# Two tiles at a time in seven half-size products, in a grouped expert GEMM followed by a folded FFN GEMM

## The reference

```python
# x: (128, 64, 1024), ids: (128,), weight: (16, 1024, 1024), all float32
y = jnp.einsum('bsi,boi->bso', x, weight[ids])
h = jnp.einsum('bsd,nrd->nbsr', y, lora_A)                       # 8 adapters of rank 16
lora = jnp.einsum('nbsr,nor->bso', h, lora_B * (2 * lora_weights)[:, None, None])
out = x + (jnp.einsum('bsd,od->bso', y, W) + bias) + lora
```

## Time and profile before

| what | value |
|---|---|
| median of 3 runs | 1487.84 us (1487.71 to 1491.29) |
| profiled execution, its own time | 1489.22 us |
| span of its instructions | 1487.5 us |
| PE busy | 1472.7 us, 99% of the span |
| DVE busy | 797.7 us, 54% |
| ACT busy | 409.0 us, 27% |
| POOL busy | 464.6 us, 31% |
| matmul instructions | 6266 in the trace |
| moved by DMA | 258 MB, 173 GB/s over the span |

### The profile page before, as it was taken

How to read it: one execution, slowest core, us unless ns; L and a number is a source line. 1 busy time by engine, 2 the same in 40 slices (tenths; PEclk the granted TensorE clock), 3 DMA queues, 4 the chain that set the end, 5 groups by cost and what they waited for, 6 DMA issues and landing times.

```text
span 1487.5 us, 29739 instructions
## 1 busy us (share of the span) xinstructions
PE 1472.7 (99%) x6266; PEld 1177.4 (79%) x6267; DVE 797.7 (54%) x1213; ACT 409.0 (27%) x537; POOL 464.6 (31%) x651
## 2 busy tenths in 40 slices
PE   8999999999999999999999999999999999999998
PEld 4887888888888887878888888888888888888887
...
GB/s 254 325 187 236 218 222 157 198 183 194 196 215 215 154 197 197 157 248 232 184 147 149 131 141 131 148 132 143 144 135 141 137 144 136 140 145 135 140 148 103
DMA packets 172716, 258.02 MB, mean 173 GB/s; under 512 B 31616, under 2 KB 135552, under 8 KB 172672
## 3 DMA queue, kind: packets, MB, share of 16 engines
q1 hardware_dynamic: 128896, 138.62, 36.0%
q10 hardware_dynamic: 23360, 73.28, 16.7%
...
HBM read 181.93 MB, written 75.50 MB: 173 GB/s over the span
## 4 chain that ended last, share of the span: by engine, by line
PE 91%; DMA 2%; issue 2%; DVE 2%; SPq 2%; ACT 0%; POOLq 0%; DVEq 0%; POOL 0%; ACTq 0%
PE ps L844 29%; PE ps L851 29%; PE ps L848 29%; PE ps L886 2%; PE ps L889 2%; DMA w_place<-in_L_cond_weight_dram 2%; SPq L244 1%; SPq L222 1%; DVE w_lo L652 1%; DVE rows_by L587 1%; DMA x_raw<-in_x_dram 0%; DVE x_turn L683 0%; POOLq L210 0%; SPq L210 0%; ACT w_hi L422 0%
## 5 line engine op out<-in xcount | busy, mean ns | idle before, releaser
L844 PE MATMUL ps<-w_hi,x_both 128*128 (+1 forms) x2000 | 507.8, 395 | 1.1 <-issue 1.1
L851 PE MATMUL ps<-w_lo,x_both 128*128 (+1 forms) x2000 | 507.1, 395 | 0.0
L848 PE MATMUL ps<-w_hi,x_both 128*128 (+1 forms) x2000 | 507.1, 395 | 0.0
L683 DVE STREAM_TRANSPOSE x_turn<-x_raw 128x256 f32<-128x256 f32 x544 | 193.7, 414 | 515.3 <-DMA x_raw<-y_scr 456.6
L844 PEld LDWEIGHTS ps<-w_hi,x_both 128*128 128x128 f32 x2000 | 375.2, 188 | 93.9 <-issue 2.5
L848 PEld LDWEIGHTS ps<-w_hi,x_both 128*128 128x128 f32 x2000 | 375.4, 188 | 91.3
L851 PEld LDWEIGHTS ps<-w_lo,x_both 128*128 128x128 f32 x2000 | 375.4, 188 | 91.3
L222 POOL DMA_DIRECT2D x_raw<-in_x_dram x560 | 299.1, 534 | 381.3 <-DVE x_turn L683 206.8
L430 ACT ACTIVATE x_both<-x_turn 128x512 fp32r<-128x512 f32 x272 | 168.3, 631 | 770.7 <-DVE x_turn L683 702.8
L405 POOL TENSOR_TENSOR rows_by<-rows_by,w_place 128x1024 f32<-128x1024 f32 x64 | 153.2, 2394 | 620.5 <-DMA rows_by<-in_x_dram 620.5
L690 DVE TENSOR_TENSOR x_both<-x_turn,x_both 128x512 fp32r<-128x512 f32 x272 | 180.8, 691 | 91.8 <-ACT x_both L430 86.1
...
## 6 DMA issues: line engine op xcount, KB each, us to landing
...
x_raw<-in_x_dram POOLq DMA_DIRECT2D x560, 64.0 KB, 3.9
x_raw<-y_scr SPq DMA_DIRECT2D x512, 64.0 KB, 2.4
rows_by<-in_x_dram SPq DMA_DIRECT2D x128, 256.0 KB, 3.7
out_dram<-rows_by ACTq DMA_DIRECT2D x126, 256.0 KB, 3.0
...
```

The lines of the kernel that those rows point to most:

```text
L683: last = nc.vector.transpose(x_turn[h][:, :, s * TOK:(s + 1) * TOK].rearrange("p t (j m) -> p m t j", m=2), x_raw[raw][:, 2 * s:2 * s + 2, ...
L844: mm(ps[b][:, cols], x_hi[b][:, t, :], hi[t], start=t == 0, stop=False)
L848: mm(ps[b][:, cols], x_lo[b][:, t, :], hi[t], start=False, stop=False)
L851: last = mm(ps[b][:, cols], x_hi[b][:, t, :], lo[t], start=False, stop=t == KT - 1)
```

## The change

Seen as 2x2 blocks, a pair of tiles (256 rows: the even rows of four samples and the odd ones, by two halves of the contraction) is multiplied by the folded matrix (two halves of the contraction by two halves of the columns) in seven products of blocks in place of eight. The operands are A11, A12, A22 of y and four sums S1 to S4; on the other side B11, B21, B22 of the folded matrix and four sums T1 to T4. A product of blocks has 3 x 4 = 12 matmuls of the same size as before, so a pair has 84 where two tiles had 96. Each goes into a PSUM bank of its own.

- **Sums of the weights.** In 16 pieces during the first stage: POOL loads a piece of `weff` (4 loads), DVE turns it and makes four sums (`turn_piece`), ACT rounds, DVE subtracts (`split_piece`), POOL stores it to DRAM (2 stores). Between the stages SP loads the sums from there: T2 over B12, which is not needed, in 8 loads of 256 KB as soon as the folded matrix is ready and the pieces are stored; T1, T3 and T4 into the other half of `w_hi` and `w_lo` when the last slot is done, in 6 loads of 1 MB. All are made of runs of 512 bytes.
- **Operands.** Per pair DVE makes four transposes of 128x512, four sums of 128x512 and seven subtractions of 128x512; ACT rounds seven of 128x512.
- **Results.** The seven products go to four quarters of the output. ACT copies the first from PSUM (`copy_common`); DVE adds two more to it in turn (`take_common`) and five straight into `out_rows`; POOL adds the three common sums to rows in four additions of 128x512 (`add_first`, `add_second`) beside the two bias additions of 128x1024 (`add_bias`).
- **Order.** DVE turns pair p + 1 (`turn_pair`) before it takes anything of pair p, and makes the subtractions between the takes. SP's loads of y stay as they are, eight for each tile; `load_rest` has four loads for each pair after one wait for `out_stored` of the pair two before.
- The end is not cut in halves any more: the last pair is stored in four stores of 256 KB. The scratch for POOL's DMA descriptors goes from 8192 to 2048 bytes.

```diff
+    T1, T2, T3, T4 = range(4)
+    A11, A12, S2, S1, S3, S4, A22 = range(7)
...
-                sp.wait_ge(x_turned, turned)
+                if isinstance(group, int) and group == 0:
+                    sp.wait_ge(x_turned, 2 * (t + SLOTS) - (2 * RING - 2))
+                elif u % 2 == 0:
+                    sp.wait_ge(y_turned, group * 8 + (4 * (u // 2) - 4))
...
+            def load_rest(p, q, stores=None):
...
+                samples = [entry(sp, order_sample, 4 * p + s, SAMPLES - 1) for s in range(4)]
                 if stores is not None:
...
-                    sp.wait_ge(out_stored[b], stores)
-                for h in range(2):
-                    sp.dma_start(stage[b][h * TOK:(h + 1) * TOK, :], one(x, samples[h])).then_inc(rest_loaded[b], 16)
+                    sp.wait_ge(out_stored[q], stores)
+                for s in range(4):
+                    sp.dma_start(out_rows[q][s * BLK:(s + 1) * BLK, :, :],
+                                 x[bass.ds(samples[s], 1)].rearrange("a (j m) n -> (a j) m n", m=2)).then_inc(rest_loaded[q], 16)
+
...
+
+            sp.wait_ge(w_ready, ranks * CHUNKS + CHUNKS)
+            sp.wait_ge(piece_stored, 32 * PIECES)
+            for comb, held in ((comb_hi, w_hi), (comb_lo, w_lo)):
+                for c in range(CHUNKS // 2):
+                    load_comb(T2, held[:, bass.ds(par, 1), CHUNKS // 2 + c, 0:KH, :].rearrange("p a t m -> p (a t) m"),
+                              comb[c * 4:(c + 1) * 4, :, T2 * P:(T2 + 1) * P].rearrange("g p f -> p g f"))
+            load_rest(0, 0)
+
+            sp.wait_ge(x_ready, 2 * SLOTS)
+            sp.dma_start(bias_sb[:, :], bias.rearrange("(a n) -> a n", a=1).to_broadcast([P, D])).then_inc(bias_loaded, 16)
+
+            sp.wait_ge(tile_done, SLOTS)
+            for i in (T1, T3, T4):
+                for comb, held in ((comb_hi, w_hi), (comb_lo, w_lo)):
+                    at = T_AT[i] // P
+                    load_comb(i, held[:, bass.ds(other, 1), at // KT:at // KT + 2, :, :].rearrange("p a c t m -> p (a c t) m"),
+                              comb[:, :, i * P:(i + 1) * P].rearrange("g p f -> p g f"))
+            for b in range(2):
+                sp.wait_ge(stored[b], 16 * (SLOTS // 2))
+            load_rest(1, 1)
...
+                    for h in range(2):
+                        load_y(g * RING + (RING + 2 * q + h), g + 1, 2 * q + h)
+                    load_rest(g * 2 + (q + 2), q, g * 64 + 64)
+
+            with sp.Fori(0, PAIRS // 2 - 1) as g:
+                for q in range(2):
+                    out_step(g, q, False)
...
+            def load_piece(i):
+                rows = weff.rearrange("(h r) n -> r h n", h=2)[bass.ds(i * BLK, BLK), :, :]
+                for q in range(QUADS):
+                    pool.dma_start(piece_raw[BLK * q:BLK * (q + 1), :, :],
+                                   rows[:, :, q * SEG:(q + 1) * SEG]).then_inc(piece_loaded, 16)
+
+            def store_piece(i):
+                pool.wait_ge(piece_ready, i + 1)
+                for comb, held in ((comb_hi, piece_hi), (comb_lo, piece_lo)):
+                    pool.dma_start(comb[bass.ds(i, 1)].rearrange("a p f -> (a p) f"),
+                                   held[:, :, :].rearrange("p b m -> p (b m)").bitcast(f32)).then_inc(piece_stored, 16)
+
+            for b in range(RING):
+                load_x(2 * RING + b, b)
+            load_piece(0)
+            with pool.Fori(3, SLOTS // RING) as g:
                 for b in range(RING):
                     load_x(RING * g + b, b)
+                store_piece(pool.snap(g - 3))
+                pool.wait_ge(piece_stored, g * 32 - 64)
+                load_piece(pool.snap(g - 2))
...
+            def add_bias(p, q):
+                pool.wait_ge(rest_loaded[q], (p // 2 + 1) * 64 if isinstance(p, int) else p)
+                for m in range(2):
+                    nc.gpsimd.tensor_tensor(out_rows[q][:, m, :], out_rows[q][:, m, :],
+                                            bias_sb[:, :], ALU.add).then_inc(rest_biased, 1)
+
+            def add_rows(p, q, i, m, half):
+                rows = out_rows[q][:, m, half * HALF:(half + 1) * HALF]
+                nc.gpsimd.tensor_tensor(rows, rows, common[q][i][:, :], ALU.add).then_inc(common_added, 1)
+
+            def add_first(p, q):
+
+                pool.wait_ge(rest_biased, p * 2 + 2)
+                pool.wait_ge(common_copied, p + 1)
+                add_rows(p, q, 0, 0, 0)
+                pool.wait_ge(taken, p * TAKES + 2)
+                add_rows(p, q, 1, 0, 1)
+
+            def add_second(p, q):
+
+                pool.wait_ge(taken, p * TAKES + 5)
+                for half in (1, 0):
+                    add_rows(p, q, 2, 1, half)
+
+            add_bias(0, 0)
+            add_first(0, 0)
+            add_bias(1, 1)
+            add_second(0, 0)
+            with pool.Fori(0, PAIRS // 2 - 1) as g:
+                add_first(g * 2 + 1, 1)
+                add_bias(g * 64 + 128, 0)
...
+            def round_op(p, q, i):
+
+                if not isinstance(p, int) or p > 1:
+                    if i in (A11, S2):
+                        act.wait_ge(common_added, p * ADDS + {A11: 1 - 2 * ADDS, S2: -ADDS}[i])
+                elif p == 0 and i in (S4, A22):
+                    act.wait_ge(tile_done, SLOTS)
+                made = {A11: (y_turned, 1), A22: (y_turned, 2), A12: (y_turned, 4),
+                        S1: (y_summed, 1), S2: (y_summed, 2), S3: (y_summed, 3), S4: (y_summed, 4)}
...
+            def copy_common(p, q):
+                act.wait_ge(product, p * OPS + 1)
+                nc.scalar.activation(common[q][0][:, :], bank[A11], COPY).then_inc(common_copied, 1)
+
+            def store_out(p, q):
+                samples = [entry(act, order_sample, 4 * p + s, SAMPLES - 1) for s in range(4)]
+                act.wait_ge(taken, p * TAKES + TAKES)
+                act.wait_ge(common_added, p * ADDS + ADDS)
+                for s in range(4):
+                    act.dma_start(out[bass.ds(samples[s], 1)].rearrange("a (j m) n -> (a j) m n", m=2),
+                                  out_rows[q][s * BLK:(s + 1) * BLK, :, :]).then_inc(out_stored[q], 16)
+
+            def out_step(p, q, last=False):
+                copy_common(p, q)
+                if not last:
+                    for i in range(OPS):
+                        round_op(p + 1, 1 - q, i)
+                store_out(p, q)
+
+            out_step(0, 0)
+            with act.Fori(0, PAIRS // 2 - 1) as g:
+                out_step(g * 2 + 1, 1)
+                out_step(g * 2 + 2, 0)
...
+            def turn_piece(i):
+                dve.wait_ge(piece_loaded, i * (16 * QUADS) + 16 * QUADS)
+                for h in range(2):
+                    nc.vector.transpose(piece_turn[:, h, :, :].rearrange("p k (t j) -> p (k t) j", j=BLK),
+                                        piece_raw[:, h, :].rearrange("p (t i) -> p t i", i=BLK)).then_inc(piece_turned, 1)
+                dve.wait_ge(piece_turned, i * 2 + 2)
+                b11, b21, b12, b22 = [piece_turn[:, h, k, :] for h in range(2) for k in range(2)]
+                t = [piece_sum[:, k, :] for k in range(4)]
+                tt(t[T1], b12, b11, ALU.subtract).then_inc(piece_summed, 1)
+                tt(t[T3], b22, b12, ALU.subtract).then_inc(piece_summed, 1)
+                dve.wait_ge(piece_summed, i * 4 + 1)
+                tt(t[T2], b22, t[T1], ALU.subtract).then_inc(piece_summed, 1)
+                dve.wait_ge(piece_summed, i * 4 + 3)
...
+            def split_piece(i):
+                dve.wait_ge(piece_rounded, i + 1)
+                tt(piece_lo[:, :, :], piece_sum[:, :, :], piece_hi[:, :, :], ALU.subtract).then_inc(piece_ready, 1)
...
+            def turn_pair(p, q):
+
+                if not isinstance(p, int):
+                    dve.wait_ge(product, p * OPS - OPS)
+                elif p == 1:
+                    dve.wait_ge(tile_done, SLOTS)
                 else:
-                    dve.wait_ge(tile_done, SLOTS + t + 1)
-                tt(stage[t % 2][:, cols], ps[t % RING][:, cols], stage[t % 2][:, cols], ALU.add
-                   ).then_inc(out_added if half else end_added, 1)
+                    dve.wait_ge(piece_stored, 32 * PIECES)
+                for i, m, k in ((A11, 0, 0), (A22, 1, 1), (S3, 1, 0), (A12, 0, 1)):
+                    nc.vector.transpose(
+                        block[q][i][:, :, :].rearrange("p t (s j) -> p s t j", j=BLK),
+                        y_raw[q][:, :, m, k * KH * BLK:(k + 1) * KH * BLK].rearrange("p s (t i) -> p s t i", i=BLK)
+                        ).then_inc(y_turned, 1)
+                dve.wait_ge(y_turned, p * 4 + 4)
+                b = [block[q][i][:, :, :] for i in range(OPS)]
+                tt(b[S1], b[S3], b[A22], ALU.add).then_inc(y_summed, 1)
+                dve.wait_ge(y_summed, p * 4 + 1)
+                tt(b[S2], b[S1], b[A11], ALU.subtract).then_inc(y_summed, 1)
```

(75 more changed lines are left out.)

247 lines of the change are left out of this document (144 added, 103 removed).

## The result

The kernel takes 1632.08 us, the median of 4 runs (1630.42 to 1633.21); the kernel before beside it 1487.78. The ratio is 1.096 [1.094, 1.098]: slower by 9.6%, far above the range of 1489 to 1548 that was forecast. The profiled execution has a span of 1631.4 us.

What follows compares the result with a forecast made beforehand. SP's queue, at 22.7 us a pair above PE's 19.6, was to pace the second stage: 829 + 28 x 22.7, then 15.0, 1.9, 24.9 and 5.8, span 1512.2, median 1513 us; 8-in-10 range 1489 to 1548.

Steps and rivals of the forecast that it cites:

- PE's 90 us saved: Second stage: 84 matmuls a pair for 96, 19.6 us for 22.4, 90 us less PE work in all.
- Rival 3: Something larger, 512-byte packets near 66 ns each or a first stage losing its lead: 1545 us and above, chance 0.06.
- First stage. I take nothing; up to 5.: First stage: the pieces' added work, 41 us on DVE, stays covered; nothing added, up to 5 us.
- Between the stages: Turn to second stage: loading the sums takes 39 us, PE loses 33 us, y(3)'s loads begin at 829.
- The step: Second stage: SP's queue takes 22.3 to 23.5 us a pair, taken as 22.7, for 28 steps.
- The loop that the forecast worked out as 21.8: Second stage, through stores and y loads: 43.6 us for two pairs, 21.8 each, so it just doesn't bind.
- 17.6 us from y's landing to the last take: Term of the loop through the stores: DVE's and POOL's work from y landing to last take, 17.6 us.
- rival 2: Second stage: DVE and POOL hold each other up; 21.5 us for 17.6, step 23.7, median 1541 us, chance 0.30.
- SP's pace: Second stage: SP's queue, full with its own issuing, sets 22.7 us a pair, 3.1 us above PE's 19.6.
- The end: After y(31)'s loads begin: issue 15.0, landing 1.9, PE 24.9, take and four stores 5.8 us.
- PE's matmuls keep their 0.233 us.: Sign that the forecast is right: each second-stage matmul still takes 0.233 us.
- The strided operands: Second stage: moving operand of four of seven products in runs of 32; between nothing and 2.8 us a pair, taken as nothing.

Runs made afterwards that it cites:

- run 1: Changed kernel without all work on the 16 weight pieces (loads, transposes, sums, rounding, stores): 1541.4 us, ratio 1.036 to the kernel before.
- run 5: run 2 with the two stores of each piece issued by ACT instead of POOL: 1552.4 us, ratio 1.044 to the kernel before.
- run 2: Changed kernel with the piece's raw tile in its own block, its load issued after the second x load: 1565.1 us, ratio 1.052 to the kernel before.
- run 4: Changed kernel with POOL adding the bias to only 8 of 1024 columns of each row: 1593.4 us, ratio 1.071 to the kernel before.
- run 6: Changed kernel with POOL adding the next pair's bias after the present pair's last common additions: 1592.8 us, ratio 1.072 to the kernel before.
- run 12: Changed kernel plus a tail timing single DVE and POOL operations without transfers: SBUF subtraction 0.69 us alone, 1.74 beside POOL.
- run 9: run 8 with SP issuing the rest rows between the loads of a pair's two y tiles: 1489.5 us, ratio 1.001 to the kernel before.
- run 8: Changed kernel with piece's own block, piece stores on ACT, y one pair ahead and bias last: 1494.1 us, ratio 1.005 to the kernel before.
- run 13: run 9 with each pair's 16 y loads merged into 4: 1436.8 us, ratio 0.965 to the kernel before.

## Why the prediction was wrong

The direction was right: PE's 90 us saved are lost elsewhere. The time was not, and the direction came out in part by something the sum had at nothing. By the marks, the changed kernel without the first stage's 82.5 us would be at 1549.6 (an estimate), just above the range. Rival 3 named "a first stage that loses its lead", at 0.06.

- **"First stage. I take nothing; up to 5."** This step failed, with 82.5 of the 119.2 us. The pieces' work was sized well: transposes 0.77 us for two (forecast 0.7), sums 0.28 to 0.29 each, the subtraction 0.68, and runs 1 and 5 put what shows of it at 5.9 us. POOL's queue was named, "6 DMAs and a store's landing", and dismissed because x loads run slots ahead. The step asked who waits for what is *behind* the wait, and not who waits for the piece's load itself. That is DVE, in order, with everything of the stage behind it. Runs 2 and 5 take 81.6 us away by moving a buffer and two issues.
- **Between the stages**, 62.5 forecast and 68.0 measured: the size was near. Its waits are seen in TensorE's 11.5 and 8.5 us for T2 and T1, in POOL's 39.2 for the bias row, which is issued behind T2, and in DVE's 16.2 for POOL. Pair 0's last product ends at 897.3, 48.3 us after the start, for 52.6. Then DVE's last take waits 11.3 us for POOL and ends at 907.08, 58.1 us after the start, for 53.3: POOL's bias for pair 1 stands ahead of pair 0's last sums and waits 16.5 us for its rows. That is most of the 5.5 us; no run tried it.
- **The step**, 22.7 for 23.48. The term in the sum was SP's own issuing, and it was too high: the y loads of a pair with the reads between them cost 13.37 us for 15.0, the four x loads 1.84 for 2.4. SP then waits for stores. The loop that the forecast worked out as 21.8 binds. Its failed entry is 17.6 us from y's landing to the last take: from the turn (1099.66 and 1119.05 in the trace) to the last take's end it is 19.2 and 21.7, as rival 2 had said (21.5, a step of 23.7). Runs 4, 6 and 12 show the stretch and where it bites, so rival 2, at 0.30, was the mechanism of this term. That its number fits so well is in part luck: of the 21.7 us, 2.3 are POOL's wait for the x rows to land, ahead of the bias (the row at 1131.87 above), which neither the forecast nor rival 2 had.
- **SP's pace** was nevertheless real as a floor: run 9 sits on it at 21.2 us, run 8 at the same height together with DVE, and run 13 lifts it. The forecast had it 1.5 us too high.
- **The end**, 47.6 for 57.1. y(31) lands as forecast (DVE turns at 1589.67, 15.4 us on, for 16.9). Then 35.2 us pass to the last take at 1624.83, for 25.6: ACT copies A11's product at 1614.72 only, after the stores of pair 30, and DVE and POOL hand the last sums back and forth.
- **"PE's matmuls keep their 0.233 us."** Not everywhere. PE stood idle for 3.42 us, worked 1 us at the full clock, and then the granted clock fell to 0.50, from 1102.3 to 1108.3, with another 2.04 us idle within it:
```profile
1101.35 1.10 PE L1199 MATMUL ps<-w_hi,op_hi 128*128 x4 [3.42 <-ACT op_hi L675]
1102.29 1.87 PE L1201 MATMUL ps<-w_lo,op_hi 128*128 x4
1106.19 2.07 PE L1204 MATMUL ps<-w_hi,op_lo 128*128 x4 [2.04 <-DVE op_lo L969]
1109.50 1.08 PE L1201 MATMUL ps<-w_lo,op_hi 128*128 x4
```
  Four take 2.07 us for 1.08, the level of 1.2 GHz, and from 1109.5 on 1.08 again. With the gaps gone, in run 13, the clock is 1.00.
- **The strided operands** (runs of 32) cost nothing: in run 13 PE paces, and its step of 19.32 us is 0.230 us for each of 84 matmuls. (The trace has 1921 in 450 us, some 2% fewer than this step makes.)
